# A transformer-like stack on one core: the root factors at three phase seams moved between engines and steps, and unread products added

## The chip, the cores and the metric

The kernel runs on one core of a Trainium2 chip. The metric is the device time of one execution in microseconds (us); lower is better. A NeuronCore has TensorE (PE; its weight loads are shown as PEld), VectorE (DVE), ScalarE (ACT), GpSimd (POOL) and SyncE (SP), which run their own instruction streams and meet through semaphores.

## The reference, cut to what matters

64 sequences of 32 tokens with 256 features (2,048 tokens) go through six residual layers, each behind a layer norm:

```python
x = x + xattn0(layernorm(x), ctx)   # 16 heads of 16, causal
x = x + attn0(layernorm(x))         # 16 heads of 128, one shared key/value head, norms on q, k and the output
x = x + ffn0(layernorm(x))          # 256 -> 1024 -> 256, 4 of 16 blocks kept per token
x = x + xattn1(layernorm(x), ctx)   # latent attention over 257 keys
x = x + attn1(layernorm(x))         # grouped attention, 16 heads, 4 key groups
x = x + ffn1(layernorm(x))          # 8 experts, top 1
```

`layernorm` needs, for each token, a mean, a variance and the factor 1/sqrt(variance + eps). `attn0` normalises its own input once more, which the kernel folds into the same factor (`EPS_LN2`, scale 1 + eps).

## The kernel before, in words

The tokens lie in `x_sb` as 16 tiles of 128 tokens (`TILES` = 16). Each layer is a phase: one `nc.Block()` in which every engine gets its own program, and which ends for all engines together, so the next phase starts when the last of them is through. The phases are `small_attention` (first attention, `xattn0`), `shared_key_attention` (`attn0`), `block_routed_ffn` (`ffn0`), `fold_weights`, `latent_attention`, `small_attention` again (`attn1`), and the routed experts.

Inside a phase the engines run a software pipeline written out by hand: `run_steps` calls `step(i, u, live)` for i from -2 to 16 or 17, and `live(d)` says whether tile i + d exists. Tile t is turned and projected in steps before t, scored in step t, weighed in step t + 1, and its residual is added in step t + 2 (in `small_attention` and `shared_key_attention`) or t + 1 (in `block_routed_ffn`). Steps 16 and 17 are a drain in which only tiles 14 and 15 are left.

The layer norm between two phases is spread over both. After a residual, `Moments.take` (L112) takes the row statistics of the tile (`bn_stats`). `Moments.roots` (L115) then forms the factors for a range of tiles on VectorE: one `bn_aggr` for each tile (L121), one `tensor_scalar` for the variance (L124), and the chain in `Root` (L175 to L192), a bit trick and three Newton rounds, each instruction waiting on a semaphore for the one before (`Link`). For one tile that are 12 waits with the statistics, for several 14 or 15 (the square takes two instructions). Before the change:

- `xattn0` calls it in VectorE's step 16 for tiles 0 to 14 (`ALL_BUT_LAST`), after `residual(14)` and after `front.selector` (a cast, L674), and ahead of step 17, which holds `outs_ready(15)` (L541, L544) and `residual(15)` (L550).
- `attn0` calls it at the head of VectorE's step 17, ahead of `out_statistics(15)` (L927); its own first steps form the factor of tile 15 (`LAST`), with the statistics of that tile.
- `ffn0` forms the factor of tile 15 in its step -1, and `fold_weights` forms all 16 for the next phase.

On TensorE the last steps of `xattn0` are: step 16 `turn_exps(15)` (L369), `turn_outs(14)` (L389), `finish(14)` (L396), `weigh(15)` (L380); step 17 `turn_outs(15)`, `finish(15)`, and then two unread products (L425). In `attn0` step 15 ends with `weigh(15)` (L787), the rest of `finish(14)` and `finish(15)` (L795), and then `keep_busy(3)` (L802). `keep_busy` multiplies the identity by constants, 512 columns at a time, into a bank that nobody reads. In `ffn0` step 15 ends with `spread(15)` (L1078), the mask for tile 15; VectorE's `apply_mask(15)` (L1169) follows, and step 16 has `down(15)` (L1087), which waits for it. The phases `attn0` and `ffn0` begin with `keep_busy(1)` (L802, L1109). In the trace an f32 product shows as two matmuls.

## Time and profile before

| what | value |
|---|---|
| three timed runs, median (lowest to highest) | 1223.96 us (1221.45 to 1233.77) |
| the profiled execution, its own time | 1219.28 us |
| the profiled execution, span | 1217.2 us |
| outside the span (1219.28 - 1217.2) | 2.1 us |
| PE busy | 1140.7 us (94%) |
| DVE busy | 706.1 us (58%) |
| ACT busy | 462.7 us (38%) |
| POOL busy | 279.5 us (23%) |
| mean granted TensorE clock | 0.962 of full |

All rows are of one profiled execution. Starts are us from the start of the span. The granted clock is a share of full speed (1.00 is 2.4 GHz, 0.50 is 1.2 GHz); between the two levels a figure is a mean over the stretch. A busy PE is not a PE at its peak.

### The profile page before, as it was taken

How to read it: one execution, taken by the hardware profiler on the slowest of the kernel's cores; microseconds unless marked ns; L12 is line 12 of the kernel's file. 1: busy time of each engine (PE TensorE's matmuls, PEld its weight loads, DVE VectorE, ACT ScalarE, POOL GpSimd, SP SyncE). 2: the span in 40 equal slices, each digit the busy share in tenths (PEclk: the TensorE clock that was granted, in tenths of full speed). 3: DMA queues.
4: the chain of work that ended last, by engine and by line, in shares of the span. 5: the costliest groups of instructions: out<-in, count | busy, mean ns of one | idle time of the engine just before them, and what ended most of it. 6: DMA issues, size and time to landing. Idle time of an engine off the chain costs nothing. (4 is left out here: it accounts for less than half of the span.)

```text
span 1217.2 us, 32616 instructions
## 1 busy us (share of the span) xinstructions
PE 1140.7 (94%) x12615; PEld 880.3 (72%) x12616; DVE 706.1 (58%) x1815; ACT 462.7 (38%) x1347; POOL 279.5 (23%) x360
## 2 busy tenths in 40 slices
PE   7997999999999989999978999999998997889997
PEld 5775888788788678887966777777666885446664
DVE  6896645545545555554248888888785885212222
ACT  2452534435334121211035565565553662022221
POOL 1700000000000000000243554554523540422222
PEclk9898999999999989999679999999999998799999
DMA  8621000000000085000101121111144552122221
GB/s 261 187 62 25 1 1 0 0 0 0 0 0 1 1 228 136 0 0 1 36 10 41 43 53 43 35 52 48 33 127 128 143 138 81 53 51 46 36 40 14
DMA packets 69948, 65.54 MB, mean 54 GB/s; under 512 B 32768, under 2 KB 60832, under 8 KB 69372
## 3 DMA queue, kind: packets, MB, share of 16 engines
q1 hardware_dynamic: 61916, 45.32, 14.9%
q0 software_dynamic: 7968, 19.32, 5.5%
q8 instruction: 45, 0.74, 0.2%
q14 instruction: 19, 0.16, 0.0%
HBM read 52.34 MB, written 13.19 MB: 54 GB/s over the span
## 5 line engine op out<-in xcount | busy, mean ns | idle before, releaser
L1660 ACT ACTIVATE xattn_exps<-xattn_ps_s,xattn_top 128x256 f32<-128x256 f32 x256 | 118.0, 475 | 78.0 <-DVE xattn_top L1728 78.0
L741 PEld LDWEIGHTS attn_ps_q<-attn_xnT,w_b_q 128*128 128x128 f32 x1024 | 118.8, 193 | 12.6 <-issue 12.6
L741 PE MATMUL attn_ps_q<-attn_xnT,w_b_q 128*128 128x128 f32 x1024 | 123.4, 276 | 0.0
L1227 POOL TENSOR_TENSOR fold_last_cos<-raw_last,all_consts 64x64 f32<-64x64 f32 x1 | 0.3, 314 | 525.2 <-POOLq L1039 525.2
L795 PE MATMUL attn_ps_out<-w_b_o,attn_oT 128*128 128x256 f32 x480 | 106.5, 380 | 1.8 <-DVE all_x L976 1.5
L795 PEld LDWEIGHTS attn_ps_out<-w_b_o,attn_oT 128*128 128x128 f32 x480 | 90.0, 190 | 15.1 <-DVE all_x L976 2.4
L849 ACT COPY attn_qT<-attn_ps_q 128x512 f32<-128x512 f32 x64 | 38.0, 594 | 148.2 <-PE attn_ps_q L741 148.2
L1735 DVE STREAM_TRANSPOSE xattn_expsT<-xattn_exps 128x1024 f32<-128x1024 f32 x64 | 79.4, 1241 | 21.4 <-ACT xattn_exps L1660 21.4
L1725 DVE TENSOR_REDUCE xattn_raw_top<-xattn_ps_s 128x4 f32<-128x1024 f32 x64 | 77.8, 1216 | 14.2 <-PE xattn_ps_s L1552 14.1
L1552 PE MATMUL xattn_ps_s<-xattn_kT,xattn_qT 64*32 64x256 f32 x2048 | 69.5, 381 | 2.9 <-ACT xattn_exps L1660 2.9
L1562 PE MATMUL xattn_ps_o<-xattn_expsT,xattn_kv 32*64 32x256 f32 x2048 | 63.6, 380 | 4.6 <-DVE xattn_last_scores L1771 3.9
L927 DVE BATCH_NORM_STATS2 attn_out_stats<-attn_ps_out 128x6 f32<-128x256 f32 x15 | 6.5, 432 | 103.3 <-PE attn_ps_out L795 103.3
L1527 PEld LDWEIGHTS xattn_ps_o<-xattn_xnT,all_d_a 128*128 128x128 f32 x512 | 60.9, 195 | 6.2 <-issue 6.2
L1527 PE MATMUL xattn_ps_o<-xattn_xnT,all_d_a 128*128 128x128 f32 x512 | 65.0, 281 | 0.0
L1070 PE MATMUL ffn_ps_h<-ffn_xnT,all_c 128*128 128x128 f32 x512 | 63.4, 284 | 0.0
L1087 PE MATMUL ffn_ps_out<-all_c,ffn_masked 128*128 128x256 f32 x256 | 61.4, 388 | 1.6 <-DVE ffn_masked L1169 1.6
L1590 PE MATMUL xattn_ps_o<-all_d_b,xattn_ctxT 128*128 128x256 f32 x240 | 55.4, 384 | 6.5 <-POOL xattn_ctxT L1478 4.8
L1562 PEld LDWEIGHTS xattn_ps_o<-xattn_expsT,xattn_kv 32*64 32x64 f32 x2048 | 44.4, 131 | 23.3 <-issue 11.2
L1070 PEld LDWEIGHTS ffn_ps_h<-ffn_xnT,all_c 128*128 128x128 f32 x512 | 60.8, 198 | 0.0
L2022 POOL DMA_INDIRECT out<-experts_y_out,experts_about x23 | 35.8, 1558 | 108.7 <-ACT experts_y_out L2094 107.0
L2104 DVE COPY experts_hT<-experts_ps_h 128x512 f32<-128x512 f32 x23 | 15.9, 692 | 68.4 <-PE experts_ps_h L2051 68.4
L1590 PEld LDWEIGHTS xattn_ps_o<-all_d_b,xattn_ctxT 128*128 128x128 f32 x240 | 44.4, 190 | 14.3 <-issue 6.8
(329 smaller groups left out, 2338.9 us busy)
## 6 DMA issues: line engine op xcount, KB each, us to landing
xattn_inverse<-xattn_inverse_rows SPq DMA_DIRECT2D x30, 256.0 KB, 4.1
all_c<-in_ctx SPq DMA_DIRECT2D x64, 64.0 KB, 1.9
moe_gate<-in_f_gate SPq DMA_DIRECT2D x8, 512.0 KB, 8.4
moe_up<-in_f_up POOLq DMA_DIRECT2D x8, 512.0 KB, 4.6
moe_down<-in_f_down POOLq DMA_DIRECT2D x8, 512.0 KB, 4.9
sorted_x<-all_zeros SPq DMA_DIRECT2D x1, 2944.0 KB, 16.3
experts_x_in<-sorted_x SPq DMA_DIRECT2D x23, 128.0 KB, 2.3
xattn_v_stage<-xattn_v_rows SPq DMA_DIRECT2D x16, 136.0 KB, 1.9
```

Source lines behind the costliest of these rows:

```text
L741: last = nc.tensor.matmul(ps_q[g % 2][:, h * P:(h + 1) * P], wq[:, c, head * DH:(head + 1) * DH], xnT[u][:, c, :], start=(c == 0), stop=(c ...
L795: last = nc.tensor.matmul(bank[:, 0:DIM], of_heads[:, h, :, :].rearrange("p b q -> p (b q)"), wo[:, h, :], start=(h == 0), stop=(h == HEAD ...
L849: nc.scalar.copy(qT[:, :, g, :].rearrange("p b (h q) -> p h b q", h=PER), ps_q[g % 2][:, :].rearrange("p (h b q) -> p h b q", h=PER, b=TB) ...
L1070: last = nc.tensor.matmul(ps_h[half][:, j * P:(j + 1) * P], w1[:, c, f * P:(f + 1) * P], xnT[:, c, :], start=(c == 0), stop=(c == KC - 1))
L1087: last = nc.tensor.matmul(ps_out[:, 0:DIM], masked[u][:, f, :], w2[:, f, :], start=(f == 0), stop=(f == chunks - 1))
L1527: last = nc.tensor.matmul(ps_q[part][:, n * P:(n + 1) * P], a_w[:, c, m * P:(m + 1) * P], xnT[:, c, :], start=(c == 0), stop=(c == KC - 1))
L1552: last = nc.tensor.matmul(ps_s[g % 2][SEQ * b:SEQ * b + SEQ, 512 * odd + nkeys * n:512 * odd + nkeys * (n + 1)], qT[u][rows, b, 2 * g + n, :],
L1562: nc.tensor.matmul(ps_o[b][64 * odd:64 * odd + 64, 0:DIM], kv[u][rows, j, :], expsT[u][rows, :, odd, :, j, :], start=(j == 0), stop=False, ...
L1590: last = nc.tensor.matmul(out_bank(t), ctxT[:, m, :, :].rearrange("p b s -> p (b s)"), b_w[:, m, :], start=(m == 0), stop=(m == pairs - 1))
L1660: nc.scalar.activation(exps[g % 2][:, nkeys * k:nkeys * (k + 1)], ps_s[g % 2][:, nkeys * k:nkeys * (k + 1)], ACT.Exp, bias=top[u][:, n:n + ...
L1725: nc.vector.tensor_reduce(of_group(raw_top), ps_s[g % 2][:, :].rearrange("p (o m n) -> p o m n", o=2, m=2), X_AXIS, ALU.max, negate=True). ...
L1735: nc.vector.transpose(expsT[u][:, g, :, :, :, :].rearrange("p o m j q -> p (o m j q)"), exps[g % 2][:, :])\
```

## The change

For the factors at the end of `xattn0` VectorE only aggregates 14 tiles (0 to 13, `aggregate`, L121) in step 16; the 14 arithmetic instructions that follow (`pool_roots`, new) run on GpSimd, each with a wait for the one before. `residual(14)` and the selector cast move to step 17. On TensorE `weigh(15)` goes ahead of `finish(14)`, and `finish(15)` waits for `residual(14)`. In `attn0` the roots, now of 14 tiles, move from the head of step 17 to the end of step 15, behind the softmax of tile 15, and the unread products at the end go from three to five. In `ffn0` two unread products go into the head of TensorE's step 16. The first steps of `attn0` and `ffn0` form the factors of tiles 14 and 15 (`LAST_TWO`) in place of tile 15 alone. In `attn1` only the count waited for changes, since tiles 13 and 14 both signal.

```diff
--- before.py
+++ after.py
@@ -47,6 +47,7 @@
 
 EPS_LN, EPS_LN2, EPS_L2 = range(3)
 ALL_BUT_LAST, LAST = range(0, TILES - 1), range(TILES - 1, TILES)
+ALL_BUT_TWO, LAST_TWO = range(0, TILES - 2), range(TILES - 2, TILES)
 
 
 class Link:
@@ -116,13 +117,34 @@
         link = Link(engine, semaphore, root.links + (3 if x is not None else 2))
         link.tile(0)
         if x is not None:
-            link(self.nc.vector.bn_stats(self.stats[:, tiles[0], :], x[:, tiles[0], :]))
+            link(self.nc.vector.bn_stats(self.stats[:, tiles[-1], :], x[:, tiles[-1], :]))
         for t in tiles:
             last = self.nc.vector.bn_aggr(self.moments[:, t, :], self.stats[:, t, :])
         link(last)
         eps = self.consts[:, C_LN + eps:C_LN + eps + 1]
         link(self.nc.vector.tensor_scalar(root.v, self.moments[:, tiles.start:tiles.stop, 1], scale, eps, ALU.mult, ALU.add))
         root(link)
+        link.end()
+
+    POOL_LINKS = 14
+
+    def aggregate(self, tiles):
+        for t in tiles:
+            last = self.nc.vector.bn_aggr(self.moments[:, t, :], self.stats[:, t, :])
+        return last
+
+    def pool_roots(self, pool, semaphore, eps, scale, tiles):
+        link = Link(pool, semaphore, self.POOL_LINKS)
+        link.tile(0)
+        g, root = self.nc.gpsimd, Root(self.nc, self.work, TILES, tiles)
+        link(g.tensor_scalar(root.v, self.moments[:, tiles.start:tiles.stop, 1], scale, self.consts[:, C_LN + eps:C_LN + eps + 1],
+                             ALU.mult, ALU.add))
+        link(g.tensor_scalar(root.y0.bitcast(I32), root.v.bitcast(I32), -0.5, float(Root.MAGIC), ALU.mult, ALU.add))
+        for y, out in ((root.y0, root.y1), (root.y1, root.y2), (root.y2, root.y3)):
+            link(g.tensor_tensor(root.b, y, root.v, ALU.mult))
+            link(g.tensor_tensor(root.a, root.b, y, ALU.mult))
+            link(g.tensor_scalar(root.b, root.a, -0.5, 1.5, ALU.mult, ALU.add))
+            link(g.tensor_tensor(out, y, root.b, ALU.mult))
         link.end()
 
     def apply(self, t, x, out):
@@ -240,6 +262,7 @@
     scores_made, scores_out, shifted_ready, exps_ready = (sem(n) for n in ("scores_made", "scores_out", "shifted_ready", "exps_ready"))
     exps_turned, expsT_ready, o_made, o_ready = (sem(n) for n in ("exps_turned", "expsT_ready", "o_made", "o_ready"))
     o_turned, oT_ready, out_made, x_ready = (sem(n) for n in ("o_turned", "oT_ready", "out_made", "x_ready"))
+    stats_taken = sem("stats_taken")
     dve_roots, dve_rest, dve_next, taken, dve_s1, dve_s2 = (sem(n) for n in ("dve_roots", "dve_rest", "dve_next", "taken", "dve_s1", "dve_s2"))
 
     with nc.Block() as block:
@@ -278,6 +301,9 @@
                 nc.gpsimd.memset(v_rows[u][:, :, :, HD], 1.0).then_inc(blank, 1)
             if cross:
                 beside(pool)
+                pool.wait_ge(xn_ready, TILES)
+                pool.wait_ge(taken, 1)
+                moments.pool_roots(pool, dve_next, EPS_LN2, 1.0 + LN_EPS, ALL_BUT_TWO)
             else:
                 loads = beside(pool)
                 for t in range(1, TILES + POOL_LEAD):
@@ -391,6 +417,8 @@
 
             def finish(t, turned_exps):
                 pe.wait_ge(oT_ready, t + 1)
+                if isinstance(t, int) and t == TILES - 1:
+                    pe.wait_ge(x_ready, t)
                 pe.wait_ge(expsT_ready, turned_exps)
                 for c in range(KC):
                     last = nc.tensor.matmul(ps_out, oT[:, c, :], w["o"][:, c, :], start=(c == 0), stop=(c == KC - 1))
@@ -409,12 +437,15 @@
                     keys_values(i + 1, 1 - u)
                     if cross:
                         queries(i + 1, 1 - u)
-                if cross and live(-2):
+                late = isinstance(i, int) and i == TILES
+                if cross and live(-2) and not late:
                     finish(i - 2, i if live(-1) else TILES)
                 if live(2):
                     turn(i + 2)
                 if live(-1):
                     weigh(i - 1, 1 - u)
+                if cross and late:
+                    finish(i - 2, TILES)
                 if cross and isinstance(i, int) and i < 1:
                     keep_busy(4)
                 if cross and isinstance(i, int) and i == 1:
@@ -549,10 +580,10 @@
                     dve.wait_ge(out_made, t + 1)
                     nc.vector.tensor_tensor(row(x_sb, t), row(x_sb, t), ps_out, ALU.add).then_inc(x_ready, 1)
                 dve.wait_ge(x_ready, t + 1)
-                if not isinstance(t, int) or t < TILES - 2:
+                if not isinstance(t, int) or t < TILES - 3:
                     moments.take(t, row(x_sb, t))
-                elif t == TILES - 2:
-                    moments.take(t, row(x_sb, t)).then_inc(taken, 1)
+                elif t < TILES - 1:
+                    moments.take(t, row(x_sb, t)).then_inc(stats_taken if cross else taken, 1)
 
             def softmax_head(t):
                 dve.wait_ge(scores_made, t + 1)
@@ -578,6 +609,11 @@
             def step(i, u, live):
                 if live(-2):
                     outs_ready(i - 2)
+                if cross and isinstance(i, int) and i == TILES:
+                    dve.wait_ge(stats_taken, 1)
+                    moments.aggregate(ALL_BUT_TWO).then_inc(taken, 1)
+                if cross and isinstance(i, int) and i == TILES + 1:
+                    residual(TILES - 2)
                 if live(2) and cross:
                     normalise(i + 2)
                     if isinstance(i, int) and i == -2:
@@ -595,20 +631,17 @@
                         queries_out(i + 1)
                     else:
                         values_out(i + 1, 1 - u)
-                if live(-2):
+                if live(-2) and not (cross and isinstance(i, int) and i == TILES):
                     residual(i - 2)
+                if cross and isinstance(i, int) and i == TILES + 1:
+                    front.selector(dve)
                 if cross and isinstance(i, int) and i == 1:
                     dve.wait_ge(front.stats_taken, 4)
                     moments.roots(dve, dve_rest, EPS_LN, 1.0, range(X_PART, TILES))
-                if cross and isinstance(i, int) and i == TILES:
-                    front.selector(dve)
-                if isinstance(i, int) and i == TILES:
+                if not cross and isinstance(i, int) and i == TILES:
                     dve.wait_ge(xn_ready, TILES)
-                    dve.wait_ge(taken, 1)
-                    if cross:
-                        moments.roots(dve, dve_next, EPS_LN2, 1.0 + LN_EPS, ALL_BUT_LAST)
-                    else:
-                        moments.roots(dve, dve_next, EPS_LN, 1.0, ALL_BUT_LAST)
+                    dve.wait_ge(taken, 2)
+                    moments.roots(dve, dve_next, EPS_LN, 1.0, ALL_BUT_LAST)
 
             run_steps(dve, step, -2, TILES + 1, 2, TILES - 3)
 
@@ -837,7 +870,7 @@
                     finish(i - 1)
 
             run_steps(pe, step, -2, TILES - 1, 2, TILES - 3)
-            keep_busy(3, ps_q[1])
+            keep_busy(5, ps_q[1])
 
         @block.scalar
         def _(act):
@@ -977,18 +1010,14 @@
                                                in1=row(x_sb, t), op0=ALU.mult, op1=ALU.add).then_inc(s["x_ready"], 1)
                 out_link.end()
                 dve.wait_ge(s["x_ready"], t + 1)
-                if not isinstance(t, int) or t < TILES - 2:
+                if not isinstance(t, int) or t < TILES - 3:
                     moments.take(t, row(x_sb, t))
-                elif t == TILES - 2:
+                elif t < TILES - 1:
                     moments.take(t, row(x_sb, t)).then_inc(s["taken"], 1)
 
             def step(i, u, live):
                 if live(2):
                     normalise(i + 2)
-                if isinstance(i, int) and i == TILES + 1:
-                    dve.wait_ge(s["xn_ready"], TILES)
-                    dve.wait_ge(s["taken"], 1)
-                    moments.roots(dve, s["dve_next"], EPS_LN, 1.0, ALL_BUT_LAST)
                 if live(-2):
                     out_statistics(i - 2)
                 if live(0):
@@ -1004,7 +1033,11 @@
                 if live(0):
                     softmax_tail(i)
                 if isinstance(i, int) and i == -1:
-                    moments.roots(dve, s["dve_roots"], EPS_LN2, 1.0 + LN_EPS, LAST, x_sb)
+                    moments.roots(dve, s["dve_roots"], EPS_LN2, 1.0 + LN_EPS, LAST_TWO, x_sb)
+                if isinstance(i, int) and i == TILES - 1:
+                    dve.wait_ge(s["xn_ready"], TILES)
+                    dve.wait_ge(s["taken"], 1)
+                    moments.roots(dve, s["dve_next"], EPS_LN, 1.0, ALL_BUT_TWO)
 
             run_steps(dve, step, -2, TILES + 1, 2, TILES - 3)
 
@@ -1089,6 +1122,8 @@
                     last.then_inc(s["out_made"], 1)
 
             def step(i, u, live):
+                if isinstance(i, int) and i == TILES:
+                    keep_busy(2, ps_h[0])
                 if live(0):
                     up(i)
                 if live(1):
@@ -1104,9 +1139,9 @@
                 if live(1):
                     route(i + 1)
 
-            def keep_busy(products):
+            def keep_busy(products, bank=ps_out):
                 for n in range(products):
-                    nc.tensor.matmul(ps_out[:, :], ident, consts[:, 0:512], start=True, stop=True)
+                    nc.tensor.matmul(bank[:, :], ident, consts[:, 0:512], start=True, stop=True)
 
             keep_busy(1)
             run_steps(pe, step, -1, TILES, 2, TILES - 2)
@@ -1185,7 +1220,7 @@
                 if live(1):
                     choose(i + 1)
                 if isinstance(i, int) and i == -1:
-                    moments.roots(dve, s["dve_roots"], EPS_LN, 1.0, LAST, x_sb)
+                    moments.roots(dve, s["dve_roots"], EPS_LN, 1.0, LAST_TWO, x_sb)
 
             run_steps(dve, step, -2, TILES, 2, TILES - 3)
 
```

## Rows read from the trace of the kernel before

**Rows 1.** The page, the span in 40 equal slices, tenths: the granted TensorE clock.

```profile
PEclk9898999999999989999679999999999998799999
```

**Rows 2.** Busy time by stretch: us, each engine (instructions), granted clock, DMA share, GB/s.

```profile
110.00:115.00 5.00, 0.69 (x2) 0.29 (x2) 3.58 (x24) 0.13 (x1) 0.00 (x0) 0.66 0.00 0
115.00:120.00 5.00, 4.26 (x10) 2.80 (x10) 0.96 (x4) 0.24 (x1) 0.00 (x0) 0.65 0.00 0
...
430.00:435.00 5.00, 3.96 (x11) 2.45 (x12) 1.25 (x5) 1.66 (x2) 0.00 (x0) 0.50 0.70 157
435.00:440.00 5.00, 5.00 (x28) 5.00 (x28) 4.32 (x18) 0.60 (x1) 0.00 (x0) 0.57 0.96 198
...
570.00:575.00 5.00, 3.45 (x14) 2.69 (x12) 1.73 (x3) 0.00 (x0) 0.00 (x0) 0.74 0.00 0
...
590.00:600.00 10.00, 10.00 (x49) 10.00 (x48) 4.10 (x30) 0.00 (x0) 3.48 (x6) 0.50 0.01 2
```

**Rows 3.** Timeline (start us, length, engine, line, idle before) of the first attention's drain.

```profile
106.03 0.44 PE L389 MATMUL xattn_ps_T<-all_consts,xattn_outs 128*128 128x128 f32 x2 [0.36 <-DVE xattn_outs L544]
...
106.93 1.13 PE L396 MATMUL xattn_ps_pT<-w_a_o,xattn_oT 128*128 128x256 f32 x4 [0.46 <-ACT xattn_oT L463]
...
107.99 0.68 PE L380 MATMUL xattn_ps_o<-xattn_v_blocks,xattn_expsT 128*32 128x68 f32 x32
...
109.49 1.08 DVE L121 BATCH_NORM_AGGREGATE all_moments<-all_row_stats 128x2 f32<-128x6 f32 x15
...
113.38 0.26 DVE L541 RECIPROCAL xattn_inverse<-xattn_ps_o 128x16 f32<-128x16 f32 x1
...
114.15 0.69 PE L389 MATMUL xattn_ps_T<-all_consts,xattn_outs 128*128 128x128 f32 x2 [5.47 <-DVE xattn_outs L544]
...
115.30 2.07 PE L396 MATMUL xattn_ps_pT<-w_a_o,xattn_oT 128*128 128x256 f32 x4 [0.46 <-ACT xattn_oT L463]
...
117.17 1.67 PE L425 MATMUL xattn_ps_kv<-all_consts 128*128 128x256 f32 x4
...
119.19 0.18 DVE L914 MEMSET attn_root_work<- 128x144 f32 x1 [1.37 <-PEq L245]
```

**Rows 4.** Timeline of GpSimd's small operations, and its 128x256 group by shape (mean ns).

```profile
578.94 0.24 POOL L1229 TENSOR_TENSOR fold_last_sin<-raw_last,all_consts 64x32 f32<-64x32 f32 x1
579.26 0.59 POOL L1232 TENSOR_TENSOR fold_last_twice<-fold_last_cos,fold_last_sin 64x64 f32<-64x64 f32 x2
...
L269 POOL TENSOR_SCALAR attn_xn<-all_x,all_moments,all_moments_work 128x256 f32<-128x256 f32 x16 | 19.5, 1220 | 46.7 <-PE attn_ps_T L312 30.2 <-POOLq L1429 16.4
```

**Rows 5.** Timeline of the shared-key attention's drain and the feed-forward's first product.

```profile
416.40 7.07 PE L795 MATMUL attn_ps_q<-w_b_o,attn_qT 128*128 128x256 f32 x32
416.60 0.43 DVE L927 BATCH_NORM_STATS2 attn_out_stats<-attn_ps_out 128x6 f32<-128x256 f32 x1 [5.73 <-PE attn_ps_out L795]
...
421.65 1.10 DVE L121 BATCH_NORM_AGGREGATE all_moments<-all_row_stats 128x2 f32<-128x6 f32 x15
...
423.31 2.74 PE L802 MATMUL attn_ps_q<-all_consts 128*128 128x512 f32 x6
...
425.56 0.43 DVE L927 BATCH_NORM_STATS2 attn_out_stats<-attn_ps_q 128x6 f32<-128x256 f32 x1
...
430.58 2.04 PE L1109 MATMUL ffn_ps_out<-all_consts 128*128 128x512 f32 x2 [4.53 <-PEq L727]
```

**Rows 6.** Timeline of the hidden products: tile 0, tile 1, and tile 0's mask.

```profile
434.39 5.83 PE L1070 MATMUL ffn_ps_h<-ffn_xnT,all_c 128*128 128x128 f32 x29
...
442.39 1.22 DVE L1169 TENSOR_TENSOR ffn_masked<-ffn_ps_mask,ffn_hidden 128x1024 f32<-128x1024 f32 x1 [2.55 <-PE ffn_ps_mask L1078]
...
442.65 3.82 PE L1070 MATMUL ffn_ps_h<-ffn_xnT,all_c 128*128 128x128 f32 x32
```

**Rows 7.** Timeline of the feed-forward's last product.

```profile
571.82 5.41 PE L1087 MATMUL ffn_ps_out<-all_c,ffn_masked 128*128 128x256 f32 x16 [1.55 <-DVE ffn_masked L1169]
```

**Rows 8.** Timeline of VectorE in the shared-key attention's first steps.

```profile
132.20 0.72 DVE L934 STREAM_TRANSPOSE attn_norms<-attn_ps_o 128x512 f32<-128x512 f32 x1 [3.56 <-PE attn_ps_o L779]
```


## Prediction

> **What bounds the kernel now.** Read the page first. TensorE is busy for 94% of the span, VectorE for 58%, and the slices of the granted clock are at 9 to full nearly everywhere [rows 1]. So in the long middle of each phase TensorE sets the time, and nothing this change does reaches it. The change touches the drains and the starts of phases, and there the shares of the page say nothing. The second view is therefore busy time by short stretches across each seam. The reader is to see two things in it: TensorE is nearly empty in 110 to 115 us (0.69 of 5 us) while VectorE is busy for 3.58; and the granted clock is low just then and afterwards, 0.66 and 0.65 up to 120 us, 0.50 and 0.57 from 430 to 440, 0.74 in 570 to 575 [rows 2]. The third view is the timeline of the seams, which says what TensorE waited for. Each drain has one plain culprit: the factors for the next layer norm, formed by VectorE ahead of work that TensorE waits for [rows 3, 5], or a mask [rows 7].
>
> **Part 1, the first attention's end.** Before, VectorE aggregates 15 tiles from 109.49 and starts tile 15's reciprocal at 113.38, though its weighing was over at 107.99 + 0.68 = 108.67. TensorE idles 5.47 us and comes back at half clock; the unread products end at 117.17 + 1.67 = 118.84 and the next phase begins at 119.19 [rows 3].
>
> After, the order on TensorE in step 16 is the turning of tile 14 (106.03 to 106.47), then the weighing of 15. That is about 0.68 us, so it ends near 107.2, and `finish(14)` takes 1.13 more, to 108.3. VectorE aggregates 14 tiles in 14/15 of 1.08 = 1.0 us from about 106.0 to 107.05, which lies beside that weighing; its reciprocal for tile 15 starts at about 107.25. From that reciprocal to the next phase it took 119.19 - 113.38 = 5.81 us before. At full clock this chain loses 0.69 - 0.44 on the turning, 2.07 - 1.13 on the last projection, and about half of the 1.67 of the unread products: 2.0 together, which leaves 3.8. `finish(14)` stands ahead of the turning and makes it 0.3 later (108.3 against 108.0). The cast that moved behind the residual (between the reciprocal's 0.26 and the aggregation's 1.08, taken as 0.7) runs beside the unread products. So TensorE and VectorE would be through for a next phase at 107.25 + 3.8 + 0.3 = 111.35.
>
> GpSimd is the other leg. It gets its signal at 107.05 and runs 14 dependent instructions on 128x14 elements. The trace has none of that shape. The nearest row below is a 64x32 product, 0.24 us, and the next one, which waits for it, starts at 579.26, 0.08 after its end: 0.32 for a link. The bound above is the 128x256 group of `tensor_scalar`, 1.22 + 0.08 = 1.30 [rows 4]. Fourteen elements lie next to 32, not 256, so I take 0.33. Then 107.15 + 14 x 0.33 = 111.8, and the next phase follows 0.35 later, as 119.19 follows the end of the unread products at 118.84: 112.15. Gain 119.19 - 112.15 = **7.0 us**, with GpSimd and the other leg nearly level. At 0.20 a link (VectorE pays 2.81 us for 13 of them between 110.57 and 113.38, 0.22 each [rows 3]) it would be 7.8, since the other leg holds at 111.35; at 1.30 it is a loss of 6.5 (107.15 + 18.2 + 0.35 = 125.7).
>
> The Trainium skill speaks against this move: GPSIMD Engine Reference, section 4.1 Engine selection, puts elementwise work on VectorE and calls GpSimd about twice as slow for two inputs. By it a link would be 2 x 0.22 = 0.44, the chain 6.2 us, the next phase at 113.7 and the gain 5.5 in place of 7.0. No row of this case shows such small tiles on both engines, so it stands as part of rival B.
>
> **Part 2, the shared-key attention's end.** The chain of 15 tiles runs from 421.65 to 425.56 = 3.9 us, while `finish(15)` on TensorE ends at 416.40 + 7.07 = 423.47; its statistics wait until 425.56 for nothing but VectorE. Moved to step 15 the chain falls into the 5.73 us in which VectorE idles before 416.60 [rows 5]: 3.9 fits, cost nothing; were that cover gone, it would cost up to 3.9 on the path of tile 14. What is late next is `finish(15)` itself: statistics at 423.5. Gain 425.56 - 423.5 = **2.05 us**. The unread products go from 6 to 10 rows of 2.74/6 = 0.46 us, so they end near 423.31 + 4.6 = 427.9. The feed-forward's first product, at 430.58 before [rows 5], would come at 430.58 - 2.05 = 428.5, after them: their cost is 0 here, and up to 0.5 if I have the end of VectorE too late.
>
> **Part 3, the clock at the feed-forward's start.** TensorE idled 4.53 us before 430.58 [rows 5] and worked at 0.50 until about 439.3 (a mean of 0.57 in 435 to 440 is 4.3 us at 0.50 and 0.7 at full [rows 2]). Now the gap is 427.9 to about 428.5. I take it that the clock stays full. Then the first unread product takes 2.74/3 = 0.91 and not 2.04 (1.1 less), the turning 0.25 less [rows 3], and 29 of tile 0's hidden products take 29/32 of 3.82 = 3.46 and not 5.83, 2.4 less [rows 6]. Gain **3.75 us**. If the clock falls all the same it is 0. The new two-tile factors on VectorE are one aggregation and three links longer, 0.07 + 3 x 0.22 = 0.75 us. In the shared-key attention they lie before an idle of 3.56 us [rows 8], cost nothing. In the feed-forward the idle before tile 0's mask is 2.55 us [rows 6]; as TensorE gets 3.75 earlier and VectorE only 1.35 (it starts from the logits), the mask would come 2.4 + 0.75 - 2.55 = 0.6 us after TensorE allows it. It is needed only after tile 1's 3.82 us of hidden products, which hide it.
>
> **Part 4, the feed-forward's end.** Before, 16 rows of the last product took 5.41 us behind an idle of 1.55 [rows 7]; at the rate of `finish(15)`, 7.07/32 = 0.221 each [rows 5], they take 3.54. If two unread products (4 x 0.46 = 1.83) in that idle hold the clock, 1.87 is won, less the 0.28 by which they overrun it: **1.6 us**. If the clock would not have fallen anyway, they cost 0.28.
>
> First the row: the clock fell in 570 to 575 though TensorE was busy 3.45 of 5 us, and it was at 0.50 in 590 to 600 though TensorE was busy all the time [rows 2]. Busy time alone thus does not hold it. The Trainium skill, TensorE: Matmul & The Clock Gate, Part 1, adds that the activity monitor runs free and does not start with the kernel, so equal instructions may keep the clock in one execution and lose it in the next. One trace cannot show that. By it part 4 is worth its 1.6 in some executions only.
>
> **The sum.** 7.0 + 2.05 + 3.75 + 1.6 = 14.4 us, so against the profiled execution 1219.28 - 14.4 = 1204.9. That execution is 4.7 us below the median of the timed runs and 2.2 below the fastest, so it had a good passage. A fall avoided is not one everywhere: I count part 4 half (0.8 less) and take off 0.4 for a clock that falls in new places (my estimate: a quarter of the executions, at the 1.87 that the fall cost in part 4). That is 13.2, and 1223.96 - 13.2 = **1210.8 us**.
>
> **The rivals.** A. The clock is lost at the feed-forward's start too. For it: low clock with a busy TensorE [rows 2], and the stretch has a gap and a few short transposes. Against: ten dense products end 0.6 us before. Part 3 goes: 1223.96 - 9.4 = 1214.6.
>
> B. GpSimd becomes the last of the first seam. From 0.30 us a link on it sets the end; at 0.50 the next phase starts at 114.5, the gain is 4.7 and the time 1213.1. For it: every row of GpSimd at 128x256 is dear [rows 4]. Against: the small ones are not.
>
> C. The slow stretch of the weight folding (0.50 at 590 to 600, TensorE fully busy [rows 2]) moves. This stretch holds on to whatever level it has, and its start is chance. Each us of it costs half a us. Entered 8 us later it gives 4 back, 1206.8; entered 8 us earlier it costs 4, 1214.8.
>
> D. Slower. GpSimd pays the fixed price of the 128x256 group on small tiles too: 1.30 a link, next phase at 125.7, which is 6.5 late. TensorE then idles 14 us and starts the shared-key attention at half clock, which costs it the 3.75 of part 3. Against parts 2 to 4, 6.2 as counted, that is +4.1: 1228.1 us. It turns slower than before at about 1.0 us a link. Against it: the 0.24 of the 64x32 product.
>
> E. That the change does not do what it says: step 16 of VectorE could find GpSimd's factors not ready for the next phase. They are not read in the drain, and the phase end waits for all engines, so this is B.
>
> **How the numbers follow.** Forecast 62%, its own range 1207 to 1214; A 11%; B 11%; C later 9%, earlier 4%; D 3%. A measurement of this kernel can tell about 1% from no change, here 12.2 us or 1211.7. Of the forecast's 62, some 47 lie below 1211.7; with C later that is 56% faster. The remaining 15, A, B, C earlier and a mild D are 42% the same, and 2% are slower. The range leaves out D and the tails of C: 1203 to 1218.
>
> **What would show it.** Right: the first phase change near 112, GpSimd's links at about 0.33 and its last ending within 0.5 us of VectorE's and TensorE's; the statistics of tile 15 in the shared-key attention right behind `finish(15)`; a granted clock of 1.00 at the feed-forward's start, with 3.8 us for tile 0's hidden products; the last product in about 3.6 us. Wrong: links over 0.4, a clock of 0.5 behind the five products, or a folding stretch longer than before by more than 2 us.

## The result and the profile after

| what | before | changed |
|---|---|---|
| timed runs | 6 | 6 |
| median (lowest to highest) | 1224.85 us (1221.2 to 1233.77) | 1214.74 us (1208.91 to 1217.2) |
| profiled execution, own time | 1219.28 us | 1214.21 us |
| its span | 1217.2 us | 1212.4 us |

The ratio is 0.989 with a 95% interval of 0.9856 to 0.9925: some 1.1% faster, with no change outside the interval. The medians alone are 10.1 us apart, 0.8%, which is inside the interval too. The forecast, 1210.8 us, lies 3.9 us below the median after, which lies inside the stated range of 1203 to 1218 and just outside the forecast's own 1207 to 1214. The page's clock slices differ from [rows 1] by a tenth in four slices, so the seams have to be read one by one. A seam is here the stretch from the last work of one phase to the first of the next, and a link is one instruction of the factor chain with its wait for the one before.

The first seam, timeline of the changed kernel (start us, length, engine, line; in brackets the idle time before and what ended it):

```profile
105.92 0.24 DVE L572 RECIPROCAL xattn_inverse<-xattn_ps_o 128x16 f32<-128x16 f32 x1
...
106.54 1.02 DVE L133 BATCH_NORM_AGGREGATE all_moments<-all_row_stats 128x2 f32<-128x6 f32 x14
...
106.68 0.44 PE L415 MATMUL xattn_ps_T<-all_consts,xattn_outs 128*128 128x128 f32 x2 [0.36 <-DVE xattn_outs L575]
...
107.75 0.28 POOL L140 TENSOR_SCALAR all_moments_work<-all_moments,all_consts 128x14 f32<-128x14 f32 x1 [54.59 <-DVE all_moments L133]
...
110.43 1.03 PE L456 MATMUL xattn_ps_kv<-all_consts 128*128 128x256 f32 x4
110.51 0.22 POOL L147 TENSOR_TENSOR all_moments_work<-all_moments_work 128x14 f32<-128x14 f32 x1
...
110.81 0.22 POOL L144 TENSOR_TENSOR all_moments_work<-all_moments_work 128x14 f32<-128x14 f32 x1
111.09 0.68 DVE L707 CAST all_sel<-all_consts 16x1024 bf16<-16x1024 f32 x1
111.10 0.74 POOL L145 TENSOR_TENSOR all_moments_work<-all_moments_work 128x14 f32<-128x14 f32 x1
...
112.23 0.22 POOL L147 TENSOR_TENSOR all_moments_work<-all_moments_work 128x14 f32<-128x14 f32 x1
113.88 0.18 DVE L947 MEMSET attn_root_work<- 128x144 f32 x1 [2.11 <-PEq L268]
...
113.97 2.05 PE L835 MATMUL attn_ps_out<-all_consts 128*128 128x512 f32 x2 [2.51 <-PEq L268]
...
118.00 4.89 PE L774 MATMUL attn_ps_q<-attn_xnT,w_b_q 128*128 128x128 f32 x32
```

GpSimd's links are 0.30 us apart, where 0.33 was forecast, but for one: the product at 111.10 takes 0.74 and not 0.22, beside VectorE's cast (0.68) that began 0.01 earlier. The last link ends at 112.45, and the next phase begins 1.43 later, at 113.88. Before, it followed TensorE's last product by 0.35 [rows 3]. Against 119.19 the phase starts 5.31 earlier; tile 14's outputs were turned 0.65 later than before (106.68 against 106.03), so the seam itself is 5.96 us shorter (5.31 + 0.65). Then TensorE, which had stood still for 2.51 us, works at half clock: its first product takes 2.05 and its first 32 query products 4.89. The kernel before, which had idled 0.45 us, took 1.10 and 3.74 here.

The two later seams, TensorE's timeline:

```profile
413.81 7.07 PE L828 MATMUL attn_ps_q<-w_b_o,attn_qT 128*128 128x256 f32 x32
420.71 4.46 PE L835 MATMUL attn_ps_q<-all_consts 128*128 128x512 f32 x10
425.94 1.10 PE L1144 MATMUL ffn_ps_out<-all_consts 128*128 128x512 f32 x2 [0.77 <-PEq L760]
...
428.18 3.82 PE L1103 MATMUL ffn_ps_h<-ffn_xnT,all_c 128*128 128x128 f32 x32
...
561.65 1.98 PE L1144 MATMUL ffn_ps_h<-all_consts 128*128 128x512 f32 x4
563.47 3.62 PE L1120 MATMUL ffn_ps_out<-all_c,ffn_masked 128*128 128x256 f32 x16
568.31 2.41 PE L1291 MATMUL fold_ps_b<-raw_o,raw_ckv 128*64 128x256 f32 x20 [1.23 <-PEq L1072]
...
609.23 0.37 PE L1333 MATMUL fold_ps_r<-all_consts,fold_last_twice 64*128 64x64 f32 x1
```

These answer to [rows 5 to 7]: the idle before the feed-forward's first product is 0.77 and not 4.53 us, tile 0's hidden products take 3.82, and the last product 3.62 and not 5.41. The last two rows are the first product and the last transposition of the weight folding, the fold.

Busy time by stretch in the fold (columns as in [rows 2]):

```profile
570.00:575.00 5.00, 5.00 (x48) 3.46 (x44) 0.66 (x2) 1.20 (x3) 0.00 (x0) 0.94 0.37 88
575.00:580.00 5.00, 5.00 (x29) 3.95 (x27) 0.63 (x2) 0.59 (x1) 2.17 (x4) 0.50 0.45 119
...
590.00:600.00 10.00, 10.00 (x49) 10.00 (x48) 3.64 (x24) 0.00 (x0) 0.00 (x0) 0.50 0.01 2
600.00:610.00 10.00, 9.59 (x45) 9.29 (x44) 1.96 (x4) 0.21 (x1) 0.00 (x0) 0.50 0.00 0
```

TensorE is busy without a break, and its clock falls to 0.50 near 574.4, 6 us into the fold. Before, it fell about 11 us in, near 589.5.

The lead of the changed execution (start before minus start after) can be followed from mark to mark:

| mark | lead, us | change |
|---|---|---|
| turning of tile 14's outputs | -0.65 | |
| shared-key attention starts (119.19, 113.88) | 5.31 | +5.96 |
| its `finish(15)` ends (423.47, 420.88) | 2.59 | -2.72 |
| feed-forward's first product (430.58, 425.94) | 4.64 | +2.05 |
| tile 1's hidden products (442.65, 434.10) | 8.55 | +3.91 |
| fold starts (578.45, 568.31) | 10.14 | +1.59 |
| fold's last transposition (615.19, 609.23) | 5.96 | -4.18 |
| end of span (1217.2, 1212.4) | 4.8 | -1.2 |

So 13.5 us were gained at the seams and 6.9 given back in two places where TensorE does the same work at half clock (2.72 and 4.18). The first row and the last lie where the edit changes nothing.

### The profile page after: what moved, and what is told of

The parts are those of the page before. It is cut to its first block and busy times, and to the rows that moved or that the text cites. A ratio compares the mean times of both kernels' runs of the same rounds, so it can differ in the third digit from the quotient of the medians.

```text
span 1212.4 us, 32639 instructions
## 1 busy us (share of the span) xinstructions
PE 1146.0 (95%) x12623; PEld 883.9 (73%) x12624; DVE 704.6 (58%) x1808; ACT 462.7 (38%) x1347; POOL 283.9 (23%) x374
```

## The experiments

To keep out what happens before the first seam, it is measured as the distance from the reciprocal of tile 14 (L572) to the next phase's `memset` (L947): 13.91 us before (105.28 to 119.19), 7.96 after (105.92 to 113.88), 5.95 less. The fold is measured from its first product to its last transposition: 36.74 before, 40.92 after. Runs 1 to 4, 5 to 8, 9 and 10, and 11 and 12 each shared a chip with runs of the kernel before, whose medians were 1224.48, 1224.48, 1224.80 and 1226.61 us.

**1. The changed kernel again.** No edit, 12 runs.

> The changed kernel again, nothing edited, to see what one execution's trace can stand for. Theory (chance): the folding stretch gave back 4.2 us in the first trace because the granted clock fell 6 us after the fold began and not 11 us after it, which is chance of the execution. Then this trace has the same seams (phase change 7.2 us after the turning of tile 14's outputs, shared-key drain and feed-forward start the same within 0.1 us) but a folding whose length from its first product to the transposition at its end differs by over 0.5 us from 40.9. Rival (cause): the new products ahead of the fold move the fall, and the length is 40.9 within 0.3 again. Time against before: 0.989, within 0.985 to 0.993.

1214.24 us (1209.1 to 1223.99), ratio 0.9935 (0.9903 to 0.9967), half a thousandth above the expected 0.985 to 0.993. The timeline of TensorE at the seam's end:

```profile
113.02 1.10 PE L835 MATMUL attn_ps_out<-all_consts 128*128 128x512 f32 x2 [2.51 <-PEq L268]
...
116.07 6.02 PE L774 MATMUL attn_ps_q<-attn_xnT,w_b_q 128*128 128x128 f32 x32
```

The seam takes 7.95 us; GpSimd ends at 111.51 and the phase begins at 112.93, 1.42 later. Behind 2.51 us of idle the first product still runs at full clock, and then the clock falls again (the 32 queries take 6.02). The fold takes 37.0 and not 40.9: the 4.2 us given back there are not in every execution of the changed kernel.

**2. The factors on VectorE after all**, in step 17 behind `residual(14)`, the order of the rest as changed.

```diff
-                moments.pool_roots(pool, dve_next, EPS_LN2, 1.0 + LN_EPS, ALL_BUT_TWO)
...
                     residual(TILES - 2)
+                    moments.roots_only(dve, dve_next, EPS_LN2, 1.0 + LN_EPS, ALL_BUT_TWO)
```

> The 14 tiles' factors back on VectorE, with all the rest of the change kept: aggregated in step 16, the chain of 13 instructions between the residual of tile 14 and that of tile 15. Theory (GpSimd's end is late by itself: the next phase began 1.43 us after its last instruction, against 0.35 after TensorE's before): VectorE's chain costs 13 x 0.22 = 2.9 us in the path, ends with the cast about 2.4 us after the cast of the changed kernel, and the phase begins 0.4 us after that: within 0.5 us of the changed kernel's, so the move to GpSimd is worth nothing and the reordering everything. Rival (the phase change itself costs 1.4 us now, whatever engine is last): the phase begins 1.4 us after VectorE's last instruction, 1.3 us later than in the changed kernel. In time both are under 0.15% of the whole and lie within the noise.

1213.91 us, ratio 0.9922 (0.989 to 0.9953). Timeline of VectorE, the first and the last of its 13 links and the seam's end, and TensorE's first product:

```profile
110.34 0.22 DVE L133 TENSOR_SCALAR all_moments_work<-all_moments,all_consts 128x14 f32<-128x14 f32 x1
...
112.89 0.17 DVE L213 TENSOR_TENSOR all_moments_work<-all_moments_work 128x14 f32<-128x14 f32 x1
...
113.55 0.68 DVE L716 CAST all_sel<-all_consts 16x1024 bf16<-16x1024 f32 x1
...
114.62 0.18 DVE L956 MEMSET attn_root_work<- 128x144 f32 x1 [0.39 <-PEq L277]
114.71 1.10 PE L844 MATMUL attn_ps_out<-all_consts 128*128 128x512 f32 x2 [2.46 <-PEq L277]
```

The seam takes 7.98 us (106.64 to 114.62), the same as with GpSimd. VectorE's leg is longer, but the phase follows its last instruction by 0.39, where it follows GpSimd's by 1.42. So the move of the chain to GpSimd is worth nothing here, and the reordering (fewer tiles aggregated, `residual(14)` and the cast behind the outputs of tile 15, `weigh(15)` first) is worth the whole 6 us. The clock stayed full in this execution behind 2.46 us of idle.

**3. Seven unread products at the seam in place of two.**

```diff
-            for n in range(2):
+            for n in range(7 if cross else 2):
                 nc.tensor.matmul(ps_kv[:, 0:DIM]
```

> Seven unread products at the first attention's end in place of two, which keeps TensorE busy for 5 x 0.43 = 2.1 us of the 2.5 that it idled before the next phase. Theory (the idle drops the clock): the granted clock stays at 1.00 through the shared-key attention's start, its first 32 query products take 3.7 us and not 4.9, and 2.7 us are won, 0.22%. Rival (the phase change is then set by TensorE, or the clock falls anyway for the sparse work around it): the phase begins later by up to 0.5 us, the clock is 0.50 at the start again and nothing is won.

1210.88 us, ratio 0.9903 (0.987 to 0.9936). The products fill the wait, idle is 0.45, the queries take 3.74, and the seam is 8.06 us. Filling costs 0.1 us here and the clock stays in this execution. The median is 3.4 us below run 1's, but the intervals overlap, so the timed runs do not show the gain.

**4. The two unread products at the feed-forward's end taken out.**

```diff
-                if isinstance(i, int) and i == TILES:
-                    keep_busy(2, ps_h[0])
```

> The two unread products ahead of the feed-forward's last product taken out, all else as in the changed kernel. Theory: the idle before the last product is 1.55 us again; where the clock falls in it, the last product takes 5.4 us and the seam is 1.6 us longer, where it does not, it takes 3.6 us and the seam is 0.3 us shorter. Over executions the mean is 0 to 1 us slower than the changed kernel. Rival (the products also set where the clock falls in the fold): the fold's length then falls back to the 36.7 of before.

1211.16 us, ratio 0.989 (0.9854 to 0.9926). TensorE's timeline:

```profile
562.05 0.61 PE L1111 MATMUL ffn_ps_mask<-ffn_maskT,all_sel 16*128 16x128 bf16 x8
564.22 5.41 PE L1120 MATMUL ffn_ps_out<-all_c,ffn_masked 128*128 128x256 f32 x16 [1.55 <-DVE ffn_masked L1202]
```

The fall of [rows 7] is back, to the hundredth. From tile 1's hidden products to the fold's start it is 135.80 us and 134.21 with the products: they are worth 1.59 us where the clock would fall. It fell in both profiles without them (before and here) and in none of the twelve with them, where the last product takes 3.62. The timed runs don't show this: the median is 3.1 us below run 1's on the same chip, not above, and the intervals overlap. The fold took 36.75 us, the rival's 36.7, but the folds with the products lie on both sides of that (35.0 to 41.0), so one execution can't tell whether the products move it.

**5. One Newton round less on GpSimd**, ten links in place of 14. The factors are less exact; nothing else is left out.

```diff
-    POOL_LINKS = 14
+    POOL_LINKS = 10
...
-        for y, out in ((root.y0, root.y1), (root.y1, root.y2), (root.y2, root.y3)):
+        for y, out in ((root.y0, root.y1), (root.y1, root.y3)):
```

> GpSimd's chain with two Newton rounds in place of three (four links fewer; the factors of tiles 0 to 13 are less exact). Theory (GpSimd alone sets the end of the first attention, and its end is 1.4 us late): its last instruction ends 4 x 0.30 = 1.2 us sooner, and the next phase begins 1.4 us after it, 1.2 us sooner than the 7.96 us from tile 14's reciprocal that the changed kernel takes, so about 6.8. Rival (the 1.4 us are not GpSimd's, something else is ready only then): the distance stays at 7.9 to 8.0.

1209.44 us, one run, so the time says little. GpSimd's last link, the cast and the next phase:

```profile
109.58 0.22 POOL L147 TENSOR_TENSOR all_moments_work<-all_moments_work 128x14 f32<-128x14 f32 x1
110.17 0.68 DVE L707 CAST all_sel<-all_consts 16x1024 bf16<-16x1024 f32 x1
111.24 0.18 DVE L947 MEMSET attn_root_work<- 128x144 f32 x1 [0.39 <-PEq L268]
```

The seam takes 6.23 us, 1.72 less than in run 1: four links of 0.30, and the 0.52 by which one link was stretched there, since this chain is over before the cast. The expected 6.8 counted the four links alone. GpSimd's leg did set the end of the seam. Now 109.80 + 1.44 and 110.85 + 0.39 are both 111.24: VectorE's leg is level with it or sets the end by itself, so this row can't give GpSimd's distance. Idle is 0.78, and the clock stays full.

**6. Unread products of 256 columns in the fold**, one behind every 16 matmuls of 64 columns or so; TensorE also waits once more, until the first group of products is copied out of the bank that takes them.

```diff
             def first_products(g, heads):
+                unread(ps_r2[1])
...
+                        if n % 8 == 0:
+                            unread(ps_b[0])
```

> Unread products of 256 columns between the small products of the weight folding: one before each group of the first products, one in each 16 rows of the second and third. Theory (the fold runs at half clock for some 34 us only because its products have too few columns for the clock, though TensorE is busy): the clock stays full for all or most of it, the second and third products take about 7 + 1.7 us each in place of 13.9, and the fold from its first product to the transposition at its end takes 26 to 29 us in place of 36 to 41; the time falls by 8 to 10 us, 0.7 to 0.8%, against the changed kernel, ratio to before 0.980 to 0.985. Rival (the clock falls there for another reason, or the added columns are too few): the clock is 0.50 again and the added products make the fold 5 to 8 us longer.

1211.11 us, ratio 0.9904 (0.9877 to 0.993). Busy time by stretch in the fold (573.61 to 604.10):

```profile
580.00:590.00 10.00, 10.00 (x85) 8.26 (x84) 2.57 (x4) 0.59 (x1) 5.54 (x8) 1.00 0.23 61
590.00:600.00 10.00, 10.00 (x83) 9.80 (x83) 5.02 (x32) 0.00 (x0) 0.00 (x0) 1.00 0.01 2
```

The clock is full here, every group of 16 products of the fold takes its full-clock time (1.57, or 1.89 to 1.90), and the fold takes 30.49 us. That is more than the expected 26 to 29 and 4.5 us below the shortest fold without them (35.0, run 8). The time fell less than expected too: 0.980 to 0.985 was expected, and the median is some 3 us below the changed kernel's (1214.03), not 8 to 10. A row of 590 to 600 with TensorE at 10.00 and the clock at 0.50 [rows 2] has become one with TensorE at 10.00 and 1.00. What differs is the kind of product, not the busy time. The added wait is in this edit too, but it leaves no idle in the rows.

**7. The same with a product behind every 8 matmuls** (the edit is against run 6).

```diff
-                    if n % 4 == 0:
+                    if n % 2 == 0:
...
-                        if n % 8 == 0:
+                        if n % 4 == 0:
```

> The same with twice as many unread products in the second and third products, one in each 8 rows. Theory: if the fewer do not always hold the clock, these do, at 2 x 1.7 us more; where the fewer do hold it, this one is 3 to 4 us slower than them: ratio to before 0.983 to 0.988. Rival (the clock falls whatever is added): the fold takes over 45 us.

1214.09 us, ratio 0.9928 (0.9902 to 0.9955). The fold takes 33.95 us, 3.5 more: the clock was held already, and the rest is only work. The expected ratio was 0.983 to 0.988, missed as in run 6; the 3 us above run 6 are as expected.

**8. Three unread products, not five, at the end of the shared-key attention.**

```diff
-            keep_busy(5, ps_q[1])
+            keep_busy(3, ps_q[1])
```

> Three unread products at the shared-key attention's end in place of five, as before the change; the earlier factors keep their place. TensorE then idles about 0.8 + 1.8 = 2.6 us before the feed-forward. Theory (it is the length of the idle that drops the clock, and 2.5 us dropped it in three of four executions at the first seam): the clock is 0.50 at the feed-forward's start in most executions, and this one most likely loses the 3.9 us that the changed kernel won there. Rival (shortening the idle from 4.5 by moving the factors was enough, the products are not needed): the clock stays at 1.00 and the seam is the same within 0.2 us.

1214.31 us, ratio 0.9929 (0.9905 to 0.9952). TensorE's timeline:

```profile
419.19 2.74 PE L835 MATMUL attn_ps_q<-all_consts 128*128 128x512 f32 x6
424.41 1.10 PE L1144 MATMUL ffn_ps_out<-all_consts 128*128 128x512 f32 x2 [2.48 <-PEq L760]
...
427.06 6.48 PE L1103 MATMUL ffn_ps_h<-ffn_xnT,all_c 128*128 128x128 f32 x32
```

The clock falls. From the start of `finish(15)` to tile 1's hidden products it is 23.36 us, and 20.29 with five products (413.81 to 434.10). In this execution moving the factors alone did not keep the clock, and all twelve profiles with five products did: part 3 hangs on those two products.

**9. The selector cast on ScalarE**, everything else as changed. The call moves from VectorE's step 17 to the end of ScalarE's program (not shown).

```diff
-        self.nc.vector.tensor_copy(self.sel16[:, :], self.consts[0:16, C_SEL:C_SEL + 1024])
+        self.nc.scalar.copy(self.sel16[:, :], self.consts[0:16, C_SEL:C_SEL + 1024])
```

> The selector cast of the first attention's last step moved from VectorE to ScalarE, nothing else. In the changed kernel one of GpSimd's 14 instructions took 0.74 us in place of 0.22 just while VectorE's cast ran. Theory (the cast, SBUF to SBUF on VectorE, shuts GpSimd out while it runs): all 14 take 0.20 to 0.28, GpSimd's chain is 0.52 us shorter, and the next phase begins 7.96 - 0.52 = 7.4 us after tile 14's reciprocal. Rival (the long one is its own, the eleventh instruction, or chance): one instruction of the chain still takes 0.7 us and the distance is 7.9 to 8.0.

1219.29 us, one run. The timeline at the cast:

```profile
110.76 1.04 ACT L707 CAST all_sel<-all_consts 16x1024 bf16<-16x1024 f32 x1
110.76 0.22 POOL L147 TENSOR_TENSOR all_moments_work<-all_moments_work 128x14 f32<-128x14 f32 x1
```

All 14 links are now of 0.20 to 0.28 us, and the seam is 7.41, 0.55 shorter. So the stretched link was the cast's doing. The seam's gain does not show in the time of this one run. Its span is 5.1 us longer than the first changed profile's, which had the same two losses, the clock behind the seam (queries 4.75 here, behind 1.96 us of idle) and a fold of 41.0 us. The difference arose at the end, where the edit changes nothing: the routing took 58.2 and not 55.0 us (first product to the first of the experts), and the experts began at half clock and took 135.7 and not 133.0 (first gate product to last product):

```profile
1073.54 3.78 PE L2079 MATMUL experts_ps_g<-moe_gate,experts_xT 128*128 x4 [0.55 <-ACT experts_xT L2122]
```

In the first changed profile this row takes 1.98. A version with both, the factors on VectorE and the cast on ScalarE, was not run. An estimate from run 2's rows: the residual ends at 113.10 + 0.42, the phase follows 0.39 later, at 113.91, and the seam is 7.3 us, as short as here without GpSimd.

**10. The parts together:** the cast on ScalarE, five unread products at the first seam, and the fold's products of run 6.

```diff
-            for n in range(2):
+            for n in range(5 if cross else 2):
                 nc.tensor.matmul(ps_kv[:, 0:DIM]
```

> The parts that won, together: the changed kernel with the cast on ScalarE, five unread products at the first attention's end in place of two, and one unread product of 256 columns in each 16 rows of the fold. Theory (the gains add): the first phase change 0.5 us sooner and the clock full behind it in most executions (1 to 2 us on average), the fold 30.5 us in place of 36 to 41 (some 6 us): 1206 us, ratio to before 0.982 to 0.987. Rival (the low stretch only moves to the next place that is thin in columns, the start of the latent attention and the routing): no faster than the version with the fold's products alone, 0.990.

1207.04 us (1203.43 to 1213.69), ratio 0.9856 (0.9823 to 0.9889). The seam and what follows:

```profile
109.61 2.32 PE L456 MATMUL xattn_ps_kv<-all_consts 128*128 128x256 f32 x10
...
110.86 0.22 POOL L147 TENSOR_TENSOR all_moments_work<-all_moments_work 128x14 f32<-128x14 f32 x1
112.51 0.18 DVE L947 MEMSET attn_root_work<- 128x144 f32 x1 [2.28 <-PEq L268]
112.60 1.10 PE L835 MATMUL attn_ps_out<-all_consts 128*128 128x512 f32 x2 [0.67 <-PEq L268]
...
115.01 3.74 PE L774 MATMUL attn_ps_q<-attn_xnT,w_b_q 128*128 128x128 f32 x32
```

The seam is 7.42 us, the clock is kept, and the fold takes 30.49 us. The profiled execution took 1212.29 us, 5 more than the median. In the later small attention, of which the change touches only the semaphore counts at its end, TensorE waited 8.7 us for transfers (groups of instructions from 915 to 996 us; behind the last bar stand the idle time and what ended most of it):

```profile
L406 PE MATMUL attn_ps_o<-attn_v_blocks,attn_expsT 128*32 128x68 f32 x448 | 9.5, 224 | 8.8 <-DMA attn_v_blocks<-attn_v_stage 8.7
```

**11. The same kernel again,** no further edit, beside run 12.

> The combined version again, beside the changed kernel on the same chip. In its first trace the last small attention took 80.7 us in place of 72.4, with TensorE waiting 9.8 us for the transfers of the values. Theory (that is chance of the execution, as the fold was): 72 to 73 us here, span near 1202, the time 6 to 9 us under the changed kernel's. Rival (the earlier start makes the weight transfers meet the values' transfers every time): over 78 us again, and half of the gain is always given back.

1209.65 us (1207.68 to 1213.21), ratio 0.9862 (0.9831 to 0.9894). The seam is 7.43, the queries take 3.74, the fold 30.5, and the group that waited 8.8 us in run 10 has 0.7 us of idle: that wait is not in every execution. The median is 3.2 us below run 12's, half of the expected 6 to 9.

**12. The changed kernel a third time,** no edit.

> The changed kernel, as the comparison for the combined version in the same session and as a third trace of it. Theory (chance): the fold's length and the clock at the shared-key attention's start differ again from the first two traces (40.9 and 37.0 us; low in both), the seams set by order alone are the same within 0.1 us. Rival: they repeat the first trace.

1212.88 us (1209.86 to 1215.49), ratio 0.9886 (0.9854 to 0.9918). GpSimd's end to the next phase is 1.42 again. TensorE's timeline:

```profile
113.49 1.10 PE L835 MATMUL attn_ps_out<-all_consts 128*128 128x512 f32 x2 [2.50 <-PEq L268]
...
115.90 3.74 PE L774 MATMUL attn_ps_q<-attn_xnT,w_b_q 128*128 128x128 f32 x32
```

This time the clock stayed full behind 2.50 us of idle, and the fold took 35.95.

The combined kernel beats the kernel before by 1.4% in both comparisons. Against the changed kernel the intervals overlap in part; on the same chip its median is 3.2 us lower, and over all runs the medians are 1209.05 (12 runs) and 1214.03 (24).

## Why the prediction was right or wrong

**The whole.** The time lies within the stated range. Parts 2, 3 and 4 came for the reasons given; part 1 came by another half of the edit than the one it was priced on. The forecast gain was 13.2 us against the median; the medians give 10.1 in the first comparison, and the interval 9.2 to 17.6, so the timed runs alone can't say that 3 us are missing. The profiles can: 14.4 us were forecast for this pair, and the execution's own time fell by 5.1. The difference, 9.3, is 1.0 at the first seam, 2.7 by the clock behind it, 4.2 in the fold, and the 0.65 and 1.2 in the rows that the edit leaves alone, less 0.4 in small terms. That the median comes so close owes something to chance, since the fold and the clock behind the seam differ from execution to execution.

**Part 1, the first seam: the mechanism right, the end mis-sized.** GpSimd's link was taken at 0.33 and is 0.30. The step that failed is "and the next phase follows 0.35 later, as 119.19 follows the end of the unread products": that row is TensorE's, and behind GpSimd it is 1.42 to 1.43 us in the ten profiles in which GpSimd ends last alone. In run 3 TensorE's unread products end last again (117.02, and the phase at 117.37), and in run 5 VectorE's leg is level. 13.91 - 7.96 = 5.95 stands for the forecast 7.0. The end came 1.08 us later than taken (1.43 against 0.35), and that is the whole gap: the chain as such took 4.70 us (107.75 to 112.45) against 14 x 0.33 = 4.62, since the 0.52 of the stretched link and the shorter links cancel. GpSimd was the last of the seam, and not nearly level with the other leg: VectorE's and TensorE's last instructions ended at 111.77 and 111.46, 0.7 and 1.0 us before GpSimd's. So rival B happened, by another price than the one it named. Part 1 was also put down to the wrong half of the edit: run 2 has the same seam without GpSimd.

From the Trainium skill (GPSIMD Engine Reference, section 4.1 Engine selection), which calls two-input elementwise work about twice as slow on GpSimd, the prediction had estimated 0.44 a link. The measurement decides: 0.30 against the 0.21 at which VectorE's links on the same 128x14 elements follow each other in run 2, 1.4 times and not two.

**What the new idle costs at the clock: under-sized.** The prediction took off 0.4 us for "a quarter of the executions, at the 1.87 that the fall cost in part 4". It did not ask how long TensorE idles at the new first seam. It is 2.5 us, and behind it the clock fell in seven of nine profiles. From the phase's start to the end of `finish(15)` these seven took 305.6 to 307.2 us and the others 304.2 to 304.3, so a fall cost 1.3 to 2.9 us (2.7 in the first profile). An estimate from the nine: 1.7 us on average, not 0.4.

| idle of TensorE at the first seam | clock fell behind it | stayed full |
|---|---|---|
| 1.96 to 2.51 us | after, 1, 4, 6, 7, 8, 9 | 2, 12 |
| 0.45 to 0.78 us | | before, 3, 5, 10, 11 |

At the feed-forward's start the clock stayed behind 0.76 to 0.78 us of idle in all twelve executions with five products, and it fell behind 2.48 us in run 8. Rival A, put at 11%, did not happen.

**Parts 2, 3 and 4: right.** The statistics of tile 15 start at 420.92, 0.04 behind the end of `finish(15)`: 2.05 us as forecast. Part 3 gave 3.91 where 3.75 was forecast (among it 0.94 on the first product, and 2.34 on the hidden products, of which all 32 took 6.16 before); run 8 shows that the two added products are what earns it (3.07 us in that pair). Part 4 gave 1.59, forecast 1.6; run 4 undoes it and loses 1.59. Counting it half was caution that the profiles did not bear out.

**Rival C, the fold's slow stretch.** It came 5 us earlier in the profiled execution (6 us into the fold, not 11). The stretch at half clock grew from 25.7 us (589.5 to 615.2) to 34.8 (574.4 to 609.2), and at the rival's half a us for each that is 4.6; measured 4.18. Rival C earlier, put at 4%, thus happened in this execution, and so did a sign that the prediction had named for being wrong, a fold over 2 us longer than before. The others show chance, as the rival said: 37.0, 36.1, 35.7, 36.8, 37.6, 35.0, 41.0 and 36.0 us (runs 1 to 5, 8, 9 and 12) where the fold was left as it is, against 36.7 before. The rival's "holds on to whatever level it has" is half right: in each of these folds the low level stayed to the end, but the full level it began with was always lost. What the prediction did not see is that the loss can be avoided: run 6 holds the clock there. The rule cited ahead from the Trainium skill (TensorE: Matmul & The Clock Gate, Part 1: The HAM clock gate, that the monitor runs free of the kernel) fits runs 1 and 12: the same kernel, the same 2.5 us of idle at the same work, and another clock behind it.

**Rival D** needed links of about 1.0 us; none of GpSimd's instructions took over 0.76, and only one of the 14 was long.

## What to carry to other kernels

When a chain moves to another engine at a phase's end, count what the phase change itself takes behind that engine, and price the reordering alone as its own version: here the move added nothing. A shorter drain gives part of its gain back if TensorE idles in what is left of it and comes back at half clock, as behind 2 to 2.5 us here; unread products into that idle cost 0.1 us. A busy TensorE is not a sign of a full clock: where it does long series of 64-column products, read the clock row, and try a few wide unread products among them.

## What the runs showed of the hardware that was not expected

- Where GpSimd is last, the next phase starts 1.42 to 1.43 us after its last instruction (after, runs 1, 4 and 6 to 12), where VectorE is last 0.39 (run 2), where TensorE is last 0.35 ([rows 3], run 3). Why is open; only the distances were measured.
- A GpSimd `tensor_tensor` of 128x14 f32 took 0.74 to 0.76 us in place of 0.22 when VectorE's cast of 16x1024 f32 to bf16 (0.68 us) began within 0.01 us of it (after, runs 1, 3, 4, 6 to 8 and 12), and 0.22 beside the same cast on ScalarE (runs 9 to 11). The Trainium skill, SBUF — State Buffer, section Who interferes with whom, has this as an exclusive lock: a VectorE cast can take the port pair that it shares with GpSimd, and whoever comes second waits it out, while ScalarE waits on nobody. The traces agree: 0.22 + 0.52 is the link plus most of the cast. Which of the two was first the rows do not tell, since their starts differ by 0.01 us at most.
- In the fold TensorE is busy all the time and its clock falls all the same, about 6 us in in the first changed profile, 11 before, later still in others. With one 256-column product per 16 matmuls of 64 columns it is full to the end (runs 6, 10 and 11), and the fold takes 30.5 us in all three.
- Executions of one kernel lie up to 15 us apart (1209.1 to 1223.99 in run 1). Two sources were seen in the profiles: where the clock falls (behind the first seam, in the fold, in the routing and at the experts' start, as in run 9), and waits for small transfers as in run 10. They were not summed up to the 15 us.
